# A four-layer graph network: the stages on both sides of the attention round in node rows, and the third layer on raw rows

## The reference

```python
x = _layernorm(x + L0(x))   # two relational convolutions, 16 edge types: mean per (target, type), then a 128x128 matrix per type
x = _layernorm(x + L1(x))   # attention: h = x @ lin_w.T, 8 heads, softmax over a target's edges, its own loop included, then proj_w and a layer norm
x = _layernorm(x + L2(x))   # W_r = sum_b w_comp[r, b] basis_w[b], 8 types; agg = segment_sum((x @ W_type)[src], dst)
                            # h = relu(agg + x @ loop_w + bias) + relu(x @ res_w + res_b); normalised over the nodes
x = _layernorm(x + L3(x))   # two convolutions: mean of x[src], two matrices each
```

## Time and profile before

| what | value |
|---|---|
| median of three timed runs | 7345.84 us (7341.05 to 7346.5) |
| profiled execution, its own time | 7340.86 us |
| span of the profiled execution | 7339.0 us |
| mean granted TensorE clock | 0.712 |
| transfers | 392,640 packets, 532 MB |

### The profile page before, as it was taken

How to read it: one execution, slowest core, us unless ns; L and a number is a source line. 1 busy time by engine, 2 the same in 40 slices (tenths; PEclk the granted TensorE clock), 3 DMA queues, 4 the chain that set the end, 5 groups by cost and what they waited for, 6 DMA issues and landing times.

```text
span 7339.0 us, 109206 instructions
## 1 busy us (share of the span) xinstructions
PE 4325.2 (59%) x22583; PEld 3700.9 (50%) x22584; DVE 2032.6 (28%) x7424; ACT 2472.4 (34%) x6738; POOL 4875.9 (66%) x5177
## 2 busy tenths in 40 slices
PE   4588888778787766666678444333444444444444
PEld 3477777677777545555544333333343434333333
DVE  6543333333333266666533100001100001000001
ACT  0122222222222244444422433333433333333333
POOL 2177777677777377777600677776677776777777
PEclk6699999999999766665657665656656566565665
DMA  2166666422222133333202222221222222222222
GB/s 68 45 163 156 161 153 159 104 53 53 53 53 53 39 89 86 85 85 85 67 0 115 74 52 52 51 52 45 62 52 52 52 51 62 53 52 52 51 52 57
DMA packets 392640, 532.00 MB, mean 72 GB/s; under 512 B 132897, under 2 KB 289986, under 8 KB 392130
## 3 DMA queue, kind: packets, MB, share of 16 engines
q0 software_dynamic: 159744, 330.88, 18.1%
q1 hardware_dynamic: 228258, 194.85, 10.2%
q10 hardware_dynamic: 4128, 1.75, 0.1%
HBM read 479.85 MB, written 47.23 MB: 72 GB/s over the span
## 4 chain that ended last, share of the span: by engine, by line
POOL 51%; issue 27%; PE 10%; DMA 4%; DVE 4%; DVEq 2%; ACT 1%; POOLq 1%; SPq 0%; ACTq 0%
POOL GB L698 29%; POOL GB L734 10%; POOL H L734 9%; POOL H L698 3%; PE PS L1118 2%; DMA GB<-table,IDX 2%; PE PS L1305 2%; DVEq L515 1%; PE PS L1414 1%; PE PS L1169 1%; PE PS L1191 1%; DMA table<-TOUT 1%; PE PS L1197 1%; DVE OH L1688 1%; PE PS L1295 1%
## 5 line engine op out<-in xcount | busy, mean ns | idle before, releaser
L698 POOL DMA_INDIRECT GB<-table,IDX x2496 | 2358.6, 945 | 852.1 <-issue 813.1
L1118 PE MATMUL PS<-OH,GB 128*128 128x128 f32 x4992 | 1163.5, 427 | 1866.3 <-DMA GB<-table,IDX 1866.3
L1118 PEld LDWEIGHTS PS<-OH,GB 128*128 128x128 f32 x4992 | 1079.9, 328 | 1954.1 <-issue 1954.1
L1642 DVE TENSOR_TENSOR ACC<-ACC,PS 128x128 f32 x416 | 118.1, 284 | 2963.9 <-PE PS L1118 2963.9
L804 ACT ACTIVATE OH<-iota_w,local 128x128 f32<-128x128 f32 x2496 | 761.8, 387 | 0.0
L896 ACT COPY TOUT<-PS 128x512 f32<-128x512 f32 x832 | 487.7, 586 | 745.5 <-PE PS L1305 744.9
L734 POOL DMA_INDIRECT GB<-in_x,IDX x416 | 401.4, 965 | 370.8 <-ACT IDX L878 236.3
L698 POOL DMA_INDIRECT GB<-table_gat,IDX x416 | 417.8, 1004 | 127.6 <-issue 124.9
L734 POOL DMA_INDIRECT GB<-table,IDX x416 | 395.5, 951 | 157.9 <-issue 157.9
L698 POOL DMA_INDIRECT H<-table_gat,IDX x416 | 409.5, 984 | 126.8 <-issue 123.1
L734 POOL DMA_INDIRECT H<-in_x,IDX x416 | 407.0, 978 | 126.8 <-issue 126.5
(11 more groups left out here) (324 smaller groups left out, 6442.5 us busy)
## 6 DMA issues: line engine op xcount, KB each, us to landing
H<-one_over SPq DMA_DIRECT2D x416, 128.0 KB
WR<-one_over SPq DMA_DIRECT2D x416, 128.0 KB
GB<-table,IDX POOLq DMA_INDIRECT x2912, 2.5
TOUT<-local_row SPq DMA_DIRECT2D x104, 256.0 KB
table<-TOUT SPq DMA_DIRECT2D x50, 512.0 KB, 2.7
GB<-in_x,IDX POOLq DMA_INDIRECT x416
H<-in_x,IDX POOLq DMA_INDIRECT x416
H<-table,IDX POOLq DMA_INDIRECT x416
```

The costliest lines, as they stand in the source:

```text
L698: pool.indirect_dma_start(out=out[:, j, :], out_offset=None, in_=r.table.dram[:, :], in_offset=bass.IndirectOffsetOnAxis(ap=idx[:, j:j + 1 ...
L1118: return nc.tensor.matmul(PS[:, bank, 0:P], GB[:, b, j * r.width:j * r.width + P], oh(b, j), **at)
L1642: return dve.tensor_tensor(dst, dst, PS[:, bank, 0:P], ALU.add)
```

## The change

The layer norm after `near_b` and everything between the attention round and the third layer's round are done in rows, in 13 groups of four blocks (the last has one). The centring matrix is multiplied into the weights beforehand. `h` is no longer recomputed but read back from `table_gat` in three transfers. DVE multiplies the turned sums by the reciprocals of the denominators (U), POOL multiplies `h` by the own weights (V), and TensorE adds both in PSUM while it transposes (UT). The work is a pipeline written out in 18 steps, in which each engine works on another group. The third layer uses raw rows, in a `near_round` with 8 types (128 columns) in place of `table8`. ACT and PE do the layer's constants before `near_b` starts, DVE's mixing moves into the batches of `near_b`. Two arrays for head masks, with nine prepared operations of DVE, go; two operations come.

```diff
+        near_c = Near(2, MIXED, table1, 0, R8, key8, HOT8, ROWS8, NEARBY8, False).after(near_b)
...
+        STEPS = range(-1, GROUPS + 4)
...
-            store_table(t_gat)
-            sp.wait_ge(*n_l0b.end())
+            for g in range(GROUPS):
+                sp.wait_ge(n0_lin, g + 1)
+                sp.dma_start(table_gat[columns_of(g), :].rearrange("(n p) w -> p n w", p=P), lin_rows(g)).then_inc(t_gat.stored[0], 16)
...
-            store_table(t_l2)
+            sp.wait_ge(r_gat.agg_free, TWO + TILES)
+            for n, (low, high) in enumerate(((0, 4), (4, 20), (20, XBLOCKS))):
+                sp.dma_start(XL[:, low * P:high * P].rearrange("p (n f) -> p n f", f=P),
+                             table_gat[low * P:high * P, 0:P].rearrange("(n p) f -> p n f", p=P)).then_inc(xl_in[n], 16)
+            for g in range(GROUPS):
+                sp.wait_ge(n1_d, AT_D["x2", g])
+                sp.dma_start(table1[columns_of(g), :].rearrange("(n p) f -> p n f", p=P),
+                             X[:, columns_of(g)].rearrange("p (n f) -> p n f", f=P)).then_inc(x2_stored, 16)
...
-            stage_table(t_gat, [sums, aux[0:2 * HEADS, :], PEN])
+            pool.wait_ge(n0_ps, GROUPS)
+            pool.memset(aux[0:2 * HEADS, :], 0.0).then_inc(gat_zeroed, 1)
+            pool.memset(sums, 0.0).then_inc(gat_zeroed, 1)
             gather_gat(r_gat)
-            stage_table(t_l2, [])
-            gather(r_l2)
+            for t in STEPS:
+                g = t
+                if 0 <= g < GROUPS:
+                    m, b = len(blocks_of(g)), g % 2
+                    rows = XL[:, columns_of(g)].rearrange("p (n h c) -> p n h c", h=HEADS, c=HD)
+                    pool.wait_ge(xl_in[xl_of(g)], 16)
+                    pool.wait_ge(n1_d, AT_D["rec", g])
+                    pool.tensor_tensor(rows, rows, OWN[b][:, 0:m, :].unsqueeze(3).to_broadcast([P, m, HEADS, HD]), ALU.mult)\
+                        .then_inc(n1_g, 1)
+            pool.wait_ge(x2_stored, 16 * GROUPS)
+            gather_near(near_c)
...
+            act.wait_ge(const_ps, 3)
+            act.copy(PZ[:, P:2 * P], PS[:, 2, 0:P])
+            act.copy(ZC[:, P:2 * P], PS[:, 2, P:2 * P]).then_inc(const_sb, 1)
...
+            for g in range(GROUPS + 1):
+                if g < GROUPS:
+                    act.wait_ge(n0_ps, g + 1)
+                    for n, q in enumerate(blocks_of(g)):
+                        ins = act.activation(unread(q), n0_centered(g, n)[:, NL:], ACT.Square, accum_out=squares[:, q:q + 1])
+                    ins.then_inc(n0_root, 1)
+                    act.wait_ge(n0_root, 2 * g + 1)
+                    here = slice(blocks_of(g)[0], blocks_of(g)[-1] + 1)
+                    act.activation(root[:, here], squares[:, here], ACT.Sqrt, bias=eps[:, 0:1], scale=1.0 / P).then_inc(n0_root, 1)
+                if g > 0:
+                    act.wait_ge(n0_inv, g)
+                    for n, q in enumerate(blocks_of(g - 1)):
+                        ins = act.activation(lin_rows(g - 1)[:, n, :], n0_products(g - 1, n), ACT.Copy,
+                                             scale=inv_root[:, q:q + 1])
+                    ins.then_inc(n0_lin, 1)
...
+            for t in STEPS:
+                g = t - 1
+                if 0 <= g < GROUPS:
+                    act.wait_ge(n1_p, AT_P["UT", g])
+                    if g >= 2:
+                        act.wait_ge(n1_p, AT_P["Z", g - 2])
+                    w = len(blocks_of(g)) * P
+                    act.activation(UT[g % 2][:, 0:w], PS[:, 4, 0:w], ACT.Identity, bias=vec("L1_gnn_gat_bias")).then_inc(n1_a, 1)
...
+            for g in range(GROUPS):
+                act.wait_ge(begin_ps, g + 1)
+                act.copy(XF[:, columns_of(g)], PS[:, g % 4, 0:len(blocks_of(g)) * P]).then_inc(begin_sb, 1)
+            for g in range(GROUPS):
+                act.wait_ge(begin_ps, GROUPS + g + 1)
+                act.activation(sums[:, columns_of(g)], PS[:, 4 + g % 4, 0:len(blocks_of(g)) * P], ACT.Identity,
+                               bias=vec("L2_gnn_bias")).then_inc(begin_sb, 1)
...
+            stage, step = near_round(near_c)
+            for c in range(FOUR):
+                stage(c, c)
+            run_near(step, PARTS_C, residual)
...
+                    pe.wait_ge(n0_lin, g - 1)
+                    pe.wait_ge(n0_x, g - 1)
+                for n, q in enumerate(blocks_of(g)):
+                    nc.tensor.matmul(n0_centered(g, n), sums[:, q * P:(q + 1) * P], CL[:, GATW:], start=True, stop=True)
+                    ins = nc.tensor.matmul(n0_products(g, n), sums[:, q * P:(q + 1) * P], CL[:, 0:GATW], start=True, stop=True)
+                ins.then_inc(n0_ps, 1)
...
+            for t in STEPS:
+                g = t - 1
+                if 0 <= g < GROUPS:
+                    pe.wait_ge(n1_d, AT_D["U", g])
+                    pe.wait_ge(n1_g, AT_G["V", g])
+                    if g >= 1:
+                        pe.wait_ge(n1_a, AT_A["UT", g - 1])
+                    for n, q in enumerate(blocks_of(g)):
+                        turned_rows = PS[:, 4, n * P:(n + 1) * P]
+                        nc.tensor.matmul(turned_rows, UB[g % 2][:, n * P:(n + 1) * P], ident[:, :], start=True, stop=False)
+                        ins = nc.tensor.matmul(turned_rows, XL[:, q * P:(q + 1) * P], ident[:, :], start=False, stop=True)
+                    ins.then_inc(n1_p, 1)
+                g = t + 1
+                if 0 <= g < GROUPS:
+                    if g >= 2:
+                        pe.wait_ge(n1_d, AT_D["U", g - 2])
+                    for n, q in enumerate(blocks_of(g)):
+                        here = slice(q * P, (q + 1) * P)
+                        nc.tensor.matmul(PS[:, 2 + g % 2, n * 2 * HEADS:(n + 1) * 2 * HEADS], aux[0:2 * HEADS, here], den_sel[:, :],
+                                         start=True, stop=True)
+                        ins = nc.tensor.transpose(PS[:, g % 2, n * P:(n + 1) * P], sums[:, here], ident[:, :])
+                    ins.then_inc(n1_p, 1)
+                g = t - 1
+                if 0 <= g < GROUPS:
+                    pe.wait_ge(n1_a, AT_A["UT", g])
+                    if g >= 1:
+                        pe.wait_ge(n1_d, AT_D["Z", g - 1])
+                    for n in range(len(blocks_of(g))):
+                        ins = nc.tensor.matmul(PS[:, 5 + n // 2, n % 2 * 2 * P:(n % 2 + 1) * 2 * P], UT[g % 2][:, n * P:(n + 1) * P], PZ,
+                                               start=True, stop=True)
+                    ins.then_inc(n1_p, 1)
+            for g in range(GROUPS):
+                pe.wait_ge(n1_d, AT_D["x2", g])
+                if g >= 4:
+                    pe.wait_ge(begin_sb, g - 3)
+                for n, q in enumerate(blocks_of(g)):
+                    ins = nc.tensor.transpose(PS[:, g % 4, n * P:(n + 1) * P], X[:, q * P:(q + 1) * P], ident[:, :])
+                ins.then_inc(begin_ps, 1)
+            for g in range(GROUPS):
+                pe.wait_ge(begin_sb, g + 1 if g < 4 else GROUPS + g - 3)
+                here = columns_of(g)
+                nc.tensor.matmul(PS[:, 4 + g % 4, 0:here.stop - here.start], mat("L2_gnn_loop_w"), XF[:, here],
+                                 start=True, stop=True).then_inc(begin_ps, 1)
...
+            dve.wait_ge(r_gat.agg_free, TWO + TILES)
+            for t in STEPS:
+                g = t
+                if 0 <= g < GROUPS:
+                    m, b = len(blocks_of(g)), g % 2
+                    dens = PS[:, 2 + b, 0:m * 2 * HEADS].rearrange("p (n h) -> p n h", h=2 * HEADS)
+                    dve.wait_ge(n1_p, AT_P["T", g])
+                    if g >= 2:
+                        dve.wait_ge(n1_g, AT_G["V", g - 2])
+                    dve.tensor_scalar(DEN[b][:, 0:m, :], dens[:, :, 0:HEADS], 1e-30, None, ALU.max).then_inc(n1_d, 1)
+                    dve.wait_ge(n1_d, AT_D["rec", g] - 2)
+                    dve.reciprocal(REC[b][:, 0:m, :], DEN[b][:, 0:m, :]).then_inc(n1_d, 1)
+                    dve.wait_ge(n1_d, AT_D["rec", g] - 1)
+                    dve.tensor_tensor(OWN[b][:, 0:m, :], dens[:, :, HEADS:], REC[b][:, 0:m, :], ALU.mult).then_inc(n1_d, 1)
+                    if g >= 2:
+                        dve.wait_ge(n1_p, AT_P["UT", g - 2])
+                    dve.tensor_tensor(UB[b][:, 0:m * P].rearrange("p (n h c) -> p n h c", h=HEADS, c=HD),
+                                      PS[:, b, 0:m * P].rearrange("p (n h c) -> p n h c", h=HEADS, c=HD),
+                                      REC[b][:, 0:m, :].unsqueeze(3).to_broadcast([P, m, HEADS, HD]), ALU.mult).then_inc(n1_d, 1)
+                g = t - 2
+                if 0 <= g < GROUPS:
+                    m = len(blocks_of(g))
+                    dve.wait_ge(n1_p, AT_P["Z", g])
+                    if g >= 2:
+                        dve.wait_ge(n1_a, AT_A["sq", g - 2])
+                        dve.wait_ge(n1_d, AT_D["y", g - 2])
+                    dve.tensor_tensor(ZB[g % 2][:, 0:m, :],
```

(21 more changed lines are left out.)

618 lines of the change are left out of this document (242 added, 376 removed).

## The result

The changed kernel takes **7007.24 us**, the median of four runs (6998.25 to 7018.23), against 7343.44 (7340.36 to 7346.5) for the kernel before, measured beside it: ratio 0.9543, 95% interval 0.9526 to 0.9559. The forecast was 7010. The profiled execution took 6998.25 us, span 6996.4, so 342.6 us less than the profiled one of before; the sum of the prediction was -332.

What follows compares the result with a forecast made beforehand. POOL bounds the rounds; between them it idles, so time saved there counts whole. -2 + 5 - 35 - 298 - 6 + 4 = -332 from 7340.9 gives 7009, stated as 7010 us; range 6970 to 7080.

Steps and rivals of the forecast that it cites:

- The stretch: From the attention round's last sum to the third round's first gather: 102 us instead of 400, a gain of 298 us.
- Transposes and denominators 0.6: PE's small operations in each pipeline step before the third round: 0.6 us at the high clock, 1.2 at the low.
- DVE's sum, 5.0: DVE's operations on one group in the pipeline before the third round: 5.0 us, the longest sum, setting the step.
- a sign of being wrong: In the pipeline before the third round: DVE and PE showing waits on each other in each step would refute the forecast.
- Fill, steps and drain: The pipeline before the third round: fill 14 us, ten steps of 5.0, drain 11, in all 75.
- The part after them: After the pipeline, ACT's copies, PE's products with `loop_w`, last copy and indices: 22 us, plus 5 for hand-overs.
- The high clock: PE in the pipeline runs at the high clock after the first steps; low-clock rival about 7065 us, chance 0.15.
- steps one after another: Rival: pipeline steps before the third round don't overlap, 14 us each, ten cost 90 more; 7100 us, chance 0.06.
- The shared port: In the pipeline, POOL's V doesn't delay DVE's U and Z; if V slips onto y or x2, +7 us.
- After `near_b`: Layer norm and table after `near_b`: PE and ACT take turns of 6.0 us; -35 us, between -27 and -48.
- Constants: The layer's constants made between the root sums and `near_b`'s first gather: +5 us, 4 to 7.
- The third round: Raw rows with four buffers shorten POOL's gather period: -6 us for the round, and +4 us for its tail.

## Why the prediction was right

- **The bound** was read rightly: of the 343 us that the profiled pair differs by, some 325 lie between the rounds and 9 in the third round. The stretch was forecast at 102 us and took 100.6, ending at 3725.0 against 3727.
- **Inside the stretch two terms were off and cancelled by luck.** "Transposes and denominators 0.6" is the one that was mis-sized: it measured 2.23 us a step, since a denominator product of 16 rows and 16 columns takes 0.32 us and a transpose beside it 0.26. DVE's sum, 5.0, was too large by 0.5. So the step was 5.83 and not 5.0, and PE set it, not DVE, against "DVE the fullest engine". The run with turned denominators and the one with a second U show it from both sides. Half of a sign of being wrong came true: DVE waits for PE in each step, though PE not for DVE. Fill, steps and drain took 83.0 us for the forecast's 75 (13.1, 57.1 and 12.9 for 14, 50 and 11). The part after them was forecast at 22 and 5 of reserve and took 17.6: the transposes for XF began at 3702.74, before the last x2, and the 13 products with `loop_w` took 10.69 us with the clock high from the first. Had only one of the two been wrong, the forecast would still have been within its range.
- **The high clock** came as argued: 1.00 in the steps, with PE full. The run without overlap shows the other branch, PE half busy, 0.61 to 0.66 and 20 us a group. But a full PE does not have the high clock at once: at the start of the pipeline it was low for 19 us in one profile. The rival "steps one after another" was the right danger, at twice the price that it had: it counted 14 us a step and no fall of the clock, 7100, where 7187.85 was measured.
- **The shared port.** V (1.06 us) runs beside U and into Z's sum, and neither gets longer: U 0.68, as in a group of the run with turned denominators where V starts only after it, and Z's sum 1.23, as in the drain. POOL's addition runs beside `y`, and `y` goes from 1.14 to 1.70, 0.56 a step, near the 0.53 that the prediction had priced for V on y or x2; the operation held up ends 0.15 us after POOL's. By the rule of the Trainium skill (SBUF — State Buffer, Who interferes with whom) that the prediction weighed, `y` with two inputs in SBUF and a POOL instruction that reads SBUF exclude each other; by that rule, the trace agrees.
- **After `near_b`** the alternation of PE and ACT was right: each turn has PE waiting 2.6 us for L922. Its size was taken between the clocks, 6.0, and the clock fell to the low level after the first turns, so 6.7: -30.5 instead of -35, inside the -27 to -48.
- **Constants**: from `near_a`'s last sum to `near_b`'s first gather it took 17.5 us (1364.67 to 1382.15) and takes 23.05, +5.6 for a forecast of +5. Nothing hid them, and the run with the indices first shows that they could be hidden.
- **Start**: `near_a`'s last gather starts at 1344.0 to 1347.1 in ten profiles, against 1349.8 before. The forecast of the preparation was -2, and it is there: the first gather after the long pause of POOL that `near_a` has behind its first 32, starts at 336.5 to 338.4 in these ten against 339.6. The rest, 0.5 to 3.6 us, lies within the round's other gathers and isn't explained. With it the first gather of `near_b` came 1.8 us earlier and not 3 later.
- **The third round**: -6 forecast for four buffers, -9 measured, and for another reason: seven pauses of POOL that the new loop doesn't have. This step of the argument was wrong though its sum was near.
- **Two sums of the prediction don't come out.** 7345.84 - 332 is 7014 and not 7010 (the 5 us between median and profiled execution were named and not added), and the stretch without its reserve of 5 gives -303 and not -308. Neither bears on the outcome.

The median fell by 336 us where the profiled pair fell by 343, for the profiled execution of the changed kernel is the fastest of its four. Its attention round took 1079.6 us from first to last gather, that of before 1079.5. In nine other profiles, of kernels that leave the attention round alone, it took 1083.0 to 1095.4, while `near_b` took 1043.4 to 1044.5 in all ten. So that round holds most of the spread; the start of the pipeline adds up to 5 us. Whether the change lengthens it on average by some 8 us can't be told from one profile of before.

## What to carry to other kernels

When a pipeline of several engines replaces separate stages, price each engine's step in full, the small operations above all: four products of 16 rows cost more here than the 128-row transposes beside them. Then ask which engine has no gap: it sets the step, and here, being TensorE, it had the high clock as well. Take an engine's own work from operations that follow each other without waiting, not from a step in which it waited. And look at what an engine's program puts in front of the four copies that release the next round: twice here some microseconds stood on the path only by order, and an order of squares and copies cost 37 us.

## What the runs showed of the hardware that was not expected

- Gathers of the attention round make most of the spread, at the same granted TensorE clock there, 0.61 to 0.62. In the profiled changed kernel 58 pairs are over 1.45 us apart, 37 us in excess; in the run with groups one by one it is 88 pairs and 53 us. POOL's own busy time there is 827.04 and 841.01 us for the same 832 gathers. What makes them longer isn't shown.
- The chip with a median of 9249.01 us for before. The records from it show PE idle before single products in the rounds' loops, with nothing to wait for, as here in `near_b` of the changed kernel:

```profile
1925.96 0.38 PE L1233 MATMUL PS<-OH,GB 128*128 128x256 f32 x1 [1.34 <-issue]
...
1928.07 0.59 PE L1233 MATMUL PS<-OH,GB 128*128 128x256 f32 x1 [1.74 <-issue]
```

The batch's indices are then staged late and POOL waits for them: 354 us for ACT's copies from 1850 to 3200, inside `near_b`, where in the first profile of the changed kernel it is 4.6 in all but the round's first and last 20 us. A round is no longer bound by POOL alone there, so what is gained between rounds is not the whole account. The cause of the idle time isn't known, nor whether it is that chip or that occasion.
